# Two-layer graph convolution with lookups: seven chunks of uneven size in place of five, embeddings multiplied during the histogram, base numbers in parts

## The chip, the cores and the metric

The program runs on one core of a Trainium2 chip. The metric is the device time of one execution in microseconds, lower is better.

## The reference, cut to what matters

There are 25,000 nodes with 64 features, 250,000 edges, and 102,400 lookups. The graph is random, both endpoints uniform.

```python
def gcn_conv(x, W, b, row, col, n):
    h = x @ W
    deg = in_degree(col) + 1                  # with the node's own loop
    norm = rsqrt(deg)[row] * rsqrt(deg)[col]  # over edges and loops
    return segment_sum(h[row] * norm[:, None], col, n) + b
h1 = gcn_conv(emb, W1, b1, row, col)          # 64 -> 128
lookup = gcn_conv(h1, W2, b2, row, col)       # 128 -> 64
y = lookup[r_input]
```

## The kernel before

Since nothing nonlinear stands between the layers, W1 and W2 are multiplied first (`w12`, 64 x 64), and both rounds of aggregation work on 64 features. A round gathers, for each edge, a row of a table in DRAM (`table`) and adds it into its target node in `acc`, which holds all nodes in SBUF: 196 tiles of 128 nodes, in 98 blocks of two tiles. To add by matmul, the edges are first sorted by block of their target. The edges lie as 125 partitions x 2000 columns; a "batch" of sorting is 8 columns (1000 edges).

The stages:

1. **Histogram** (L459 to L484 on ScalarE, L616 on TensorE, `digit_rows` on VectorE). For 250 batches, one-hot rows of the targets' high and low digits are made, five of eight columns' low rows by VectorE (L864) and three as sign rows by ScalarE (L463), and TensorE multiplies them (L600). This gives in-degrees and, from columns counted apart, the number of edges of each block in each column of a chunk.
2. **Base numbers** (L896 to L987, VectorE). Prefix sums over blocks for all five chunks (L912), the order of visits, the seeds of the ranks (L1007), and the roots of the degrees.
3. **Sorting.** A chunk is 50 batches (`CB`). For each batch VectorE makes block one-hots (`block_onehots`), TensorE ranks edges within blocks (`rank_before`, `rank_rest`), VectorE takes the least (`least_ranks`, L1022) and makes partition one-hots and, for each of 8 columns, a column one-hot 488 wide (`column_onehot`, L1048, `CV` = 488) in a ring of four (`TRING`). ScalarE scales the partition one-hots by two digits of the source (`scale_column`, L497). TensorE places them (`place_column`, L600, 125 x 488): two matmuls for each column, a signal (`columns_placed`) after each. At the end of a chunk `decode` and two rounds of matmuls (`turn_sources`, `pick_tiles`) turn PSUM into gather indices (`source`, L1123) and targets.
4. **Embeddings.** While chunk 0 is sorted, TensorE also multiplies embT by `w12` (L759), VectorE scales by the root of the degree (L1147), and SP writes `table[0]`.
5. **Visits.** A chunk has 391 tiles of 128 sorted edges, gathered by GpSimd, one indirect DMA per tile (L399), in batches of 8 into a ring of 16 batches (`gath`). A tile whose edges belong to two blocks is visited for each, so a chunk has up to 391 + 97 visits, 61 batches of 8 (`VB`). A visit is a target one-hot (L1059 on VectorE, L504 and L508 on ScalarE for three of eight in round 0 up to the last chunk), TensorE's product with the tile (L702, four matmul instructions), and VectorE's addition into the block (L1069). PE signals each visit (`visits_multiplied`). The planned place of each visit is read into registers from `visits`, which SP loads once. GpSimd gathers batch n only when the visits of batch n-3 of its chunk's count are done (L416, `LAG`), and TensorE waits until the tiles of a whole batch of visits have landed, which SP counts (L350).

In round 0 the visits of chunk c run beside the sorting of chunk c+1 (`both`). After chunk 0, six batches are sorted alone (`AHEAD`) while GpSimd fills its ring. 11 batches of visits per chunk run without sorting, in the last sorted chunk 17, and the 61 of chunk 4 run alone, together with the constants (L929) and ScalarE's scaling and writing of `table[1]` (L571, L575). Round 1 is 5 x 61 batches of visits. At the end GpSimd fetches 800 tiles of lookups (L432), and SP writes them out.

Of the kernel before, what the change touches and what calls it, by code (L numbers as in the profile page):

```python
# [9 lines left out]
U8 = mybir.dt.uint8  # L10
ALU = mybir.AluOpType
# [17 lines left out]
CHUNKS = 5  # L29
W8 = 8  # L30
CB = EC // CHUNKS // W8


GB = -(-(EC // CHUNKS * EP) // (P * W8))
GT = GB * W8
CV = -(-(-(-(EC // CHUNKS * EP) // P) + NB - 1) // W8) * W8
VB = CV // W8
# [10 lines left out]
STEPS = 4  # L48
LOOPED = 11
# [5 lines left out]
CREDIT = 8  # L55
VISIT_CREDIT = 2 * W8
ADD_CREDIT = 2 * W8
TRING = 4
# [5 lines left out]
TURN = 2  # L64
AHEAD = 6
# [11 lines left out]
SHARE = 4  # L77

# [3 lines left out]

assert NT % ET == 0 and CV <= RW and CB * W8 * CHUNKS == EC and CB + TURN < VB and GROUPS % 2 and (VB - GROUPS) % 2 == 0 and CHUNKS * VB % 2 and NB == HIGH and BN == LOW
assert OUT_GROUPS * OUT_GROUP == OUT_TILES and OUT_SLOTS * OUT_GROUP <= NT
assert P * NT // NIBBLE + 1 <= HALF and NIBBLE * LOW == CODE and VB <= GB + LAG and GB == CB - 1 and RANKS <= 512 and W8 % SHARE == 0
assert all(t * RECIPROCAL >> 18 == t // RINGT for t in range(CHUNKS * GT)) and CHUNKS * GT * RECIPROCAL < 1 << 23
assert max(HISTW, CHUNKS * SLOTS) <= RINGT * FEAT - SLOTS and HBUF * HIGH <= 2 * NT and RINGT <= P and CHUNKS * GB * P < 1 << 15
assert CV * P < MARK and MARK // P % RW == 0
assert CB % 2 == 0 and GROUPS == CB - 1 and LOOPED * STEPS + 4 == CB - 2


def dve_rank(k):

    return k - sum(m < k for m in ON_ACT)


def build(nc, r_input, edge_index, embT, W1T, b1, W2, b2, out):

    with ExitStack() as ctx:  # L99
# [9 lines left out]
        visits_dram = nc.dram_tensor("visits_dram", [2, CHUNKS, P * VP], I32).ap()  # L109

# [8 lines left out]
        counts = scratch[:, 0:CHUNKS * SLOTS].bitcast(F32)  # L119
# [5 lines left out]
        edge_lo = acc[:, 128:128 + 2 * EC // (2 * FEAT) + 1, :].bitcast(F16).rearrange("p t f -> p (t f)")[:, 0:2 * EC]  # L125
        ramp = sb("ramp", [P, RW], F16)
        order = sb("order", [P, BN], F16)
        zeros_f = scratch[:, RINGW - SLOTS:RINGW].bitcast(F32)
# [9 lines left out]
        lo_half = acc[:, 160:192, :].rearrange("p t f -> p (t f)")[:, 0:EC]  # L138
        ones_f = acc[:, 16:18, :].rearrange("p t f -> p (t f)")
# [140 lines left out]
        act_onehots = sem("act_onehots")  # L280
        distances = sem("distances")

        gathered = [sem(f"gathered_{which}") for which in ("even", "odd", "last")]


        landed_of = [sem(f"landed_of_{r}") for r in range(2)]
# [1016 lines left out]
```

## Time and profile before

| what | value |
|---|---|
| median of 3 executions | 9087.14 us (9071.83 to 9087.93) |
| the profiled execution's own time | 9114.78 us |
| its span, first to last instruction | 9103.6 us |
| busy over the span | PE 61%, POOL 50%, DVE 44%, ACT 26% |
| histogram / base numbers / sorting of chunk 0 | 303 / 44 / 335 us |
| first gather, first visit | 713 us, 899 us |
| round 0 from its first visit, round 1, lookups | 3620, 3471, 1114 us |

A row of a view by stages gives the stretch, its length, then each engine's busy time and its count of instructions in it, then TensorE's granted clock (1.0 is 2.4 GHz, 0.5 is 1.2 GHz), the DMA engines' share and GB/s. PEld is TensorE's loading of weights, which overlaps its matmuls. In a view by lines, "output<-inputs shape xcount | busy us, mean ns of one | idle time of the engine before them, and what ended it". "remote" and "issue" are idle time for which the profile shows no releaser.

### The profile page before, as it was taken

What the parts mean: (1) busy time and instruction counts of PE and PEld (TensorE: products, weight loads), DVE (VectorE), ACT (ScalarE), POOL (GpSimd) and SP (SyncE); (2) the same over time, 40 slices, a digit from 0 to 9 for tenths busy, and PEclk for the clock granted to TensorE, in tenths of its full rate; (3) what the DMA queues carried; (4) which work ended last, traced back from release to release, by engine and by line L of the source; (5) the groups of instructions that cost most, each with busy time, mean ns of one, the idle gap of its engine ahead of it and who ended that gap; (6) DMA issues with size and microseconds to landing.
All of it is one profiled execution on the core that took longest, in us unless ns stands there. A gap on an engine that the chain in (4) does not pass through costs nothing. (4 is left out here: it accounts for less than half of the span.)

```text
span 9103.6 us, 134830 instructions
## 1 busy us (share of the span) xinstructions
PE 5542.4 (61%) x27534; PEld 4657.6 (51%) x27535; DVE 4024.4 (44%) x13873; ACT 2331.4 (26%) x6635; POOL 4595.8 (50%) x4740
## 2 busy tenths in 40 slices
PE   8893877777777687676645576576675675700000
PEld 6441655555655555665645575575575575700000
DVE  9872755655555465354434443343343343400000
ACT  9772754655555465200000000000000000100000
POOL 0005356355355535635346536646636636467777
PEclk9996876877777687555555555555555555555555
DMA  0011011011001100111101101101101101111111
GB/s 10 14 40 20 11 19 22 11 19 20 13 19 19 20 13 19 22 23 28 25 15 21 21 14 22 22 14 22 22 14 22 22 20 30 25 46 50 46 47 45
DMA packets 203343, 211.00 MB, mean 23 GB/s; under 512 B 81404, under 2 KB 119046, under 8 KB 203200
## 3 DMA queue, kind: packets, MB, share of 16 engines
q0 software_dynamic: 151040, 154.97, 8.6%
q1 hardware_dynamic: 25360, 41.62, 1.3%
q10 hardware_dynamic: 26800, 12.88, 0.5%
q8 instruction: 44, 0.72, 0.0%
q14 instruction: 99, 0.81, 0.0%
HBM read 163.62 MB, written 45.54 MB: 23 GB/s over the span
## 5 line engine op out<-in xcount | busy, mean ns | idle before, releaser
L399 POOL DMA_INDIRECT scratch<-table,source x3920 | 3743.9, 955 | 4137.2 <-PE ps L702 1908.7
L702 PEld LDWEIGHTS ps<-scratch,late 128*128 128x128 f32 x19520 | 3988.4, 295 | 2015.3 <-issue 1866.5
L702 PE MATMUL ps<-scratch,late 128*128 x19520 | 4013.5, 379 | 1640.0 <-issue 980.9
L1069 DVE TENSOR_TENSOR acc<-acc,ps 128x128 f32 x4880 | 1371.4, 281 | 1852.9 <-issue 754.9
L1059 DVE TENSOR_SCALAR late<-order,target 128x256 f32<-128x256 f16 x4148 | 1524.5, 368 | 959.3 <-issue 787.8
L600 PE MATMUL ps<-late 125*128 125x488 f16 x4000 | 1316.4, 420 | 612.9 <-DVE late L1048 365.3
L497 ACT ACTIVATE late<-prt_onehot,scratch 125x128 f16<-125x128 f16 x4000 | 1253.2, 388 | 1140.2 <-remote 681.6
L1048 DVE TENSOR_SCALAR late<-ramp,tcol 125x488 f16<-125x488 f16 x2000 | 685.0, 349 | 817.4 <-remote 667.2
L432 POOL DMA_INDIRECT acc<-lookup,scratch x800 | 847.5, 1059 | 352.1 <-issue 243.7
L571 ACT ACTIVATE acc<-acc,dinv (+1 forms) x196 | 57.5, 340 | 3428.1 <-DVE acc L1069 3375.3
L600 PEld LDWEIGHTS ps<-late 125*128 125x128 f16 x4000 | 420.9, 128 | 719.9 <-DVE late L1048 346.8
L508 ACT ACTIVATE late<-distance,one_col 128x256 f32<-128x256 f16 x732 | 371.7, 508 | 472.3 <-remote 261.3
L504 ACT ACTIVATE distance<-order,target 128x256 f16<-128x256 f16 x732 | 362.7, 496 | 5.7 <-issue 0.5
L463 ACT ACTIVATE scratch<-ramp,acc 125x257 f16<-125x257 f16 x750 | 300.4, 503 | 0.2
L600 PE MATMUL ps<-scratch,hi_onehot 125*98 125x265 f16 x2000 | 280.4, 283 | 22.6 <-ACT dec L470 2.1
L1022 DVE TENSOR_REDUCE place_i<-ps 125x8 int32<-125x784 f32 x250 | 242.3, 969 | 98.9 <-PE ps L600 47.5
L600 PEld LDWEIGHTS ps<-scratch,hi_onehot 125*98 125x98 f16 x2000 | 216.7, 125 | 86.5 <-DVE hi_onehot L864 86.2
L864 DVE TENSOR_TENSOR prt_onehot<-ramp,prt 125x512 f16<-125x512 f16 x500 | 208.5, 417 | 39.5 <-issue 32.9
L571 ACT ACTIVATE acc<-acc,dtmp (+1 forms) x196 | 57.5, 340 | 596.1 <-DVE acc L1069 526.5
L864 DVE TENSOR_TENSOR scratch<-ramp,acc 125x1280 f16<-125x1280 f16 x250 | 204.8, 819 | 0.2 <-issue 0.2
L600 PE MATMUL ps<-blk_onehot,before 125*128 125x392 bf16 x500 | 166.4, 425 | 44.6 <-issue 38.1
L600 PE MATMUL ps<-blk_onehot,after 125*128 125x392 bf16 x500 | 140.2, 366 | 52.0 <-DVE place_i L1022 46.0
(139 smaller groups left out, 1144.4 us busy)
## 6 DMA issues: line engine op xcount, KB each, us to landing
scratch<-table,source POOLq DMA_INDIRECT x3920
out<-acc SPq DMA_DIRECT2D x40, 640.0 KB
acc<-lookup,scratch POOLq DMA_INDIRECT x800
late<-embT SPq DMA_DIRECT2D x49, 128.0 KB, 2.6
table<-acc SPq DMA_DIRECT2D x49, 128.0 KB, 2.2
table<-acc ACTq DMA_DIRECT2D x49, 128.0 KB
lookup<-acc ACTq DMA_DIRECT2D x49, 128.0 KB
acc<-edge_index SPq DMA_DIRECT2D x2, 875.0 KB
```

Source lines behind the costliest of these rows:

```text
L399: pool.indirect_dma_start(out=place, out_offset=None, in_=table[r], in_offset=bass.IndirectOffsetOnAxis(ap=source[:, t:t + 1], axis=0)).th ...
L432: pool.indirect_dma_start(out=out_rows[:, h, k, :], out_offset=None, in_=lookup, in_offset=bass.IndirectOffsetOnAxis(ap=ask_i[:, t:t + 1], ...
L463: act.activation(lo_rows[0:EP, b, j, 0:LOW + 1], ramp[0:EP, 0:LOW + 1], ACT.Sign, bias=lo_half[0:EP, bass.ds(s * W8 + j, 1)], scale=-1.0). ...
L497: act.activation(piece[0:EP, k, j, :], prt_onehot[0:EP, b, j, :], ACT.Copy, scale=digit[k][0:EP, bass.ds(s * W8 + j, 1)]).then_inc(pieces_ ...
L504: act.activation(distance[:, 0:BN], order[:, :], ACT.Abs, bias=target[:, bass.ds(g * W8 + k, 1)], scale=-1.0).then_inc(distances, 1)
L508: act.activation(target_onehot[:, odd * W8 + k, :], distance[:, 0:BN], ACT.Relu, bias=one_col[:, 0:1], scale=-1.0).then_inc(act_onehots, 1)
L600: return pe.matmul(dst, lhsT, rhs, start=False, stop=False, skip_group_check=True)
L702: last = pe.matmul(visit_ps[odd * W8 + k][:, n * FEAT:(n + 1) * FEAT], target_onehot[:, odd * W8 + k, n * P:(n + 1) * P], row, start=True, ...
L864: return dve.tensor_tensor(place.rearrange("p j (w r) -> p j w r", r=2), of_row.rearrange("p (w r) -> p w r", r=2).unsqueeze(1).broadcast_ ...
L1048: dve.tensor_scalar(tcol_onehot[E, j % TRING, :], ramp[E, 0:CV], tcol[E, b, j:j + 1], None, ALU.is_equal).then_inc(tcol_onehots, 1)
L1059: dve.tensor_scalar(target_onehot[:, odd * W8 + k, :], order[:, :], target[:, bass.ds((g - r * BATCHES) * W8 + k, 1)], None, ALU.is_equal) ...
L1069: dve.tensor_tensor(dst, dst, visit_ps[odd * W8 + k].rearrange("p (n f) -> p n f", f=FEAT), ALU.add).then_inc(visits_added, 1)
```

## The change

- **Chunks.** Seven of 24, 32, 32, 32, 40, 40 and 50 batches (`SORTED`) in place of five of 50. Tiles, gather batches and visit batches follow for each (`TILES`, `GBS`, `VBS`): 188, 250, 250, 250, 313, 313 and 391 tiles; 24, 32, 32, 32, 40, 40 and 49 batches of gathers; 36, 44, 44, 44, 52, 52 and 61 batches of visits. Only real tiles are gathered. The placing matmuls, column one-hots and the decode chain are `WIDTH[c]` = 288, 352, 416 or 488 columns wide.
- **Order.** Chunk 0 is sorted alone, then 6 batches of chunk 1, and the rest beside visits; after each later chunk 4 to 12 batches of visits run without sorting (`VISITS_AFTER`).
- **Embeddings.** TensorE multiplies units of 8 tiles in the histogram, one per 8 batches (`multiply_unit`), ScalarE copies them to `acc` (`copy_unit`), and in each span of 8 batches one sign row moves from ScalarE to VectorE. VectorE scales the table in 14 parts of 14 tiles while chunk 0 is sorted (`scale_table`, after batches 2 to 15), and SP writes them.
- **Base numbers** are worked out chunk by chunk in ten parts (`base_numbers`): those of chunk 0 inside the histogram, those of chunk c+1 while chunk c is sorted. The block counts go through DRAM and are spread to all partitions by a broadcasting DMA in place of matmuls. The visit tables of chunks 1 to 6 are stored and loaded from ScalarE's queue.
- **Signals.** `columns_placed` and `visits_multiplied` now rise once per four columns or visits, `pieces_ready` once per pair of pieces; the ring of column one-hots has eight places, and VectorE and ScalarE wait once per four columns.
- **Landings.** TensorE waits for the landing of tiles once for each half of a batch of visits.

```diff
-CHUNKS = 5
 W8 = 8
-CB = EC // CHUNKS // W8
...
+SORTED = (24, 32, 32, 32, 40, 40, 50)
+CHUNKS = len(SORTED)
+SORT0 = [sum(SORTED[:c]) for c in range(CHUNKS)]
+BATCHED = sum(SORTED)
+
+TILES = [-(-n * W8 * EP // P) for n in SORTED]
+GBS = [-(-t // W8) for t in TILES]
+GB0 = [sum(GBS[:c]) for c in range(CHUNKS)]
+GATHERS = sum(GBS)
+VBS = [-(-(t + NB - 1) // W8) for t in TILES]
+VB0 = [sum(VBS[:c]) for c in range(CHUNKS)]
+BATCHES = sum(VBS)
+GT = max(TILES)
+WIDTH = [n * W8 for n in VBS]
...
-CREDIT = 8
-VISIT_CREDIT = 2 * W8
+HALF8 = W8 // 2
+CREDIT = 2
+VISIT_CREDIT = 2 * W8 // 4
 ADD_CREDIT = 2 * W8
-TRING = 4
+TRING = 8
...
+FIRST_ALONE = 6
+VISITS_AFTER = (0, 4, 8, 10, 8, 8, 12)
+ALONE = sum(SORTED[1:]) - FIRST_ALONE + sum(VISITS_AFTER)
+UNIT = 4
+UNITS = -(-NB // UNIT)
+SPAN = 8
...
+SCALED = 14
...
+            for u in range(UNITS):
+                if u > 0:
+                    sp.wait_ge(emb_multiplied, u)
+                for h in range(2):
+                    first = (unit_block(u) + h * (NB // 2)) * BN
+                    sp.dma_start(emb_sb[h * FEAT:(h + 1) * FEAT, :], embT[:, first:first + UNIT * P]).then_inc(emb_loaded, 16)
+                if u == COUNTS_SPAN:
+                    sp.wait_ge(counts_made, 1)
+                    spread_counts(0, 1)
+                if u == BASE_SPAN:
+                    sp.wait_ge(base_step, BASE_STEPS)
+                    for a in range(2):
+                        sp.dma_start(visits_dram[a, 0].rearrange("(p k) -> p k", p=P), visit_at[:, a, 0:VP]).then_inc(visits_stored, 16)
+                    sp.wait_ge(visits_stored, 16 * 2)
+                    sp.dma_start(visits[:, 0:VBS[0] * W8], visits_dram[:, 0, 0:VBS[0] * W8]).then_inc(visits_loaded, 16)
...
+                    for k in range(real_tiles(n)):
+                        gather(gath[:, (n % RINGB) * W8 + k, :], n * W8 + k, batch)
...
+            def copy_unit(u, n):
+
+                act.wait_ge(emb_multiplied, u + 1)
+                act.copy(acc[:, :, :].rearrange("p (s t) f -> p s t f", s=2)[:, :, bass.ds(n, UNIT), :],
+                         emb_ps.rearrange("p (q s f) -> p s q f", s=2, f=FEAT)).then_inc(emb_copied, 1)
...
                 for k in range(2):
-                    act.activation(piece[0:EP, k, j, :], prt_onehot[0:EP, b, j, :], ACT.Copy,
-                                   scale=digit[k][0:EP, bass.ds(s * W8 + j, 1)]).then_inc(pieces_ready, 1)
+                    made = act.activation(piece[0:EP, k, j, :], prt_onehot[0:EP, b, j, :], ACT.Copy,
+                                          scale=digit[k][0:EP, bass.ds(s * W8 + j, 1)])
+                made.then_inc(pieces_ready, 1)
...
+                act.wait_ge(base_step, (c + 1) * BASE_STEPS + (2 if c == CHUNKS - 1 else 0))
+                for a in range(2):
+                    act.dma_start(visits_dram[a, c].rearrange("(p k) -> p k", p=P),
+                                  visit_at[:, a, c * VP:(c + 1) * VP]).then_inc(visits_stored, 16)
+                for k in range(VISITS_AFTER[c]):
+                    visit_batch(g + k, k % 2)
+                    if k == 0:
+                        act.wait_ge(visits_stored, 2 * 16 * (c + 1))
+                        act.dma_start(visits[:, VB0[c] * W8:(VB0[c] + VBS[c]) * W8], visits_dram[:, c, 0:VBS[c] * W8]).then_inc(visits_loaded, 16)
+                g += VISITS_AFTER[c]
+                act.wait_ge(decode_step, (c + 1) * DEC)
...
+            def multiply_unit(u):
+
+                pe.wait_ge(emb_loaded, u * 32 + 32)
+                pe.wait_ge(emb_copied, u + 1)
+                nodes = emb_sb.rearrange("f (g p h) -> f g h p", p=P, h=BT)
+                for q in range(UNIT):
+                    last = pe.matmul(emb_ps[:, q * 2 * FEAT:(q + 1) * 2 * FEAT], nodes[:, q // BT, q % BT, :], w12[:, :],
+                                     start=True, stop=True)
+                last.then_inc(emb_multiplied, 1)
...
-                pe.wait_ge(pieces_ready, s * (2 * W8) + (2 * j + 2 + PIECE_CREDIT))
+            def place_column(s, j, c):
+                pe.wait_ge(pieces_ready, s * W8 + (j + 1 + PIECE_CREDIT))
                 pe.wait_ge(tcol_onehots, s * W8 + (j + 1))
                 for k in range(2):
-                    last = add(place_ps[k], piece[0:EP, k, j, :], tcol_onehot[0:EP, j % TRING, :])
-                last.then_inc(columns_placed, 1)
+                    last = add(place_ps[c][k], piece[0:EP, k, j, :], tcol_onehot[0:EP, j % TRING, 0:WIDTH[c]])
+                if j % HALF8 == HALF8 - 1:
+                    last.then_inc(columns_placed, 1)
 
             place_of = [pe.alloc_register(f"place_of_{k}") for k in range(W8)]
-            needed = pe.alloc_register("needed")
+            needed = [pe.alloc_register(f"needed_{h}") for h in range(2)]
...
-                pe.reg_alu(needed, place_of[W8 - 1], (1 << 15) - P, ALU.bitwise_and)
-                pe.reg_alu(place_of[W8 - 1], place_of[W8 - 1], P - 1, ALU.bitwise_and)
-
-            def wait_landed(r):
-                pe.wait_ge(landed_of[r], needed)
+                for h in range(2):
+                    end = place_of[h * VP + VP - 1]
+                    pe.reg_alu(needed[h], end, (1 << 15) - P, ALU.bitwise_and)
+                    pe.reg_alu(end, end, P - 1, ALU.bitwise_and)
...
+                if k % VP == 0:
+                    pe.wait_ge(landed_of[r], needed[k // VP])
...
+            def scale_table(k):
+
+                tiles = slice(k * SCALED, (k + 1) * SCALED)
+                if k == 0:
+                    dve.wait_ge(emb_copied, UNITS + 1)
+                dve.tensor_tensor(acc[:, tiles, :], acc[:, tiles, :], dinv[:, tiles].unsqueeze(2).broadcast_to([P, SCALED, FEAT]),
+                                  ALU.mult).then_inc(table_scaled, 1)
...
+            def base_numbers(c, part):
+
+                n = [c * BASE_STEPS + BASE_AT[part]]
+                if part > 0:
+                    dve.wait_ge(base_step, n[0])
...
+            digit_spans(0, COUNTS_SPAN)
+            dve.wait_ge(counts_copied, 2)
+            dve.tensor_tensor(counted[:, 0, :], summed[:, 0, 0, :], summed[:, 1, 0, :], ALU.add).then_inc(counts_made, 1)
+            digit_spans(COUNTS_SPAN, BASE_SPAN)
+            for k in range(BASE_PARTS):
+                base_numbers(0, k)
+            dve.wait_ge(rank_zeroed, 1)
+            seed_ranks(0)
+            digit_spans(BASE_SPAN, BATCHED // SPAN)
...
+            def column_onehot(s, j, b, c):
+
+                if j % HALF8 == 0:
+                    dve.wait_ge(columns_placed, s * 2 + (j // HALF8 + 1))
+                dve.tensor_scalar(tcol_onehot[E, j % TRING, 0:WIDTH[c]], ramp[E, 0:WIDTH[c]], tcol[E, b, j:j + 1], None,
...
+                parts = BASE_PARTS if more else 0
+                half = (end - s - 2 - parts) // 4 * 2
+                if half > 0:
+                    with dve.Fori(0, half // 2) as i:
+                        for b in range(2):
+                            both(s + i * 2 + b, c, b, g + i * 2 + b, b)
+                for k in range(parts):
+                    both(s + half + k, c, k % 2, g + half + k, k % 2)
+                    base_numbers(c + 1, k)
```

## Rows read from the trace of the kernel before

**Rows 1.** The page: busy time of each engine in all

```profile
PE 5542.4 (61%) x27534; PEld 4657.6 (51%) x27535; DVE 4024.4 (44%) x13873; ACT 2331.4 (26%) x6635; POOL 4595.8 (50%) x4740
```

**Rows 2.** Busy time of each engine by stage (us, count of instructions, clock)

```profile
17.00:320.00 303.00, 280.10 (x1996) 216.28 (x1995) 302.95 (x500) 301.57 (x760) 0.00 (x0) 1.00 0.00 0
320.00:364.00 44.00, 10.50 (x41) 5.69 (x38) 39.54 (x63) 6.25 (x11) 0.00 (x0) 0.69 0.01 1
364.00:699.00 335.00, 320.98 (x1498) 148.28 (x1496) 250.37 (x808) 242.51 (x809) 0.00 (x0) 0.99 0.13 38
699.00:713.00 14.00, 8.51 (x20) 4.61 (x20) 7.18 (x16) 2.21 (x8) 0.00 (x0) 0.63 0.00 0
713.00:899.00 186.00, 44.20 (x133) 12.38 (x132) 30.88 (x94) 31.00 (x93) 122.19 (x128) 0.57 0.12 23
899.00:4519.00 3620.00, 2651.99 (x14092) 2140.18 (x14090) 2004.98 (x7318) 1680.55 (x4752) 1776.13 (x1841) 0.72 0.10 19
4519.00:7990.00 3471.00, 2225.38 (x9760) 2129.56 (x9760) 1380.93 (x5063) 57.34 (x196) 1845.61 (x1951) 0.50 0.10 20
```

**Rows 3.** The same view of L702's matmuls alone, in stretches of visits

```profile
1666.80:1761.60 94.80, 54.18 (x384) 56.42 (x383) 1.00 0.00 0
1790.10:2122.10 332.00, 130.18 (x768) 145.07 (x769) 0.78 0.10 19
...
4519.30:4692.60 173.30, 30.60 (x129) 31.69 (x129) 0.50 0.12 23
4692.60:4767.70 75.10, 75.10 (x354) 75.10 (x354) 0.50 0.01 2
5469.70:6005.00 535.30, 327.54 (x1408) 308.88 (x1409) 0.50 0.12 22
```

**Rows 4.** All engines, in two of these stretches of round 0

```profile
1666.80:1761.60 94.80, 91.69 (x649) 69.91 (x647) 88.63 (x335) 87.19 (x259) 0.45 (x1) 1.00 0.00 0
1790.10:2122.10 332.00, 244.52 (x1297) 179.32 (x1297) 188.29 (x673) 184.33 (x529) 184.89 (x192) 0.78 0.10 19
```

**Rows 5.** What L399 waited for (us, times), and L702

```profile
L399 POOL DMA_INDIRECT scratch<-table,source x3920: 938/944/2088, 713.1 to 7885.5; - x196
...
  PE ps L702: 1908.7, 260
  issue: 1144.7, 3537
...
  SPq L355: 4.0, 2
```

**Rows 6.** VectorE in order of time, at 7400 us and at 7656 us

```profile
7400.00 0.29 DVE L1069 TENSOR_TENSOR acc<-acc,ps 128x128 f32 x1 [0.51 <-remote]
7400.26 0.35 DVE L1059 TENSOR_SCALAR late<-order,target 128x256 f32<-128x256 f16 x1
...
7655.91 0.35 DVE L1059 TENSOR_SCALAR late<-order,target 128x256 f32<-128x256 f16 x1 [1.87 <-issue]
```

**Rows 7.** Groups by line: count, busy, mean ns, idle before and releaser

```profile
L1048 DVE TENSOR_SCALAR late<-ramp,tcol 125x488 f16<-125x488 f16 x2000 | 685.0, 349 | 817.4 <-remote 667.2 <-PE ps L600 118.0 <-issue 31.6
...
L600 PE MATMUL ps<-scratch,hi_onehot 125*98 125x265 f16 x2000 | 280.4, 283 | 22.6 <-ACT dec L470 2.1
...
L864 DVE TENSOR_TENSOR scratch<-ramp,acc 125x1280 f16<-125x1280 f16 x250 | 204.8, 819 | 0.2 <-issue 0.2
...
L864 DVE TENSOR_TENSOR hi_onehot<-ramp,scratch 125x784 f16<-125x784 f16 x250 | 140.0, 560 | 0.0
...
L902 DVE TENSOR_TENSOR seed<-identity,dec 98x784 f32<-98x784 f32 x5 | 4.5, 970 | 0.0
```

**Rows 8.** VectorE in order of time, two rank minima after chunk 0

```profile
713.23 0.97 DVE L1022 TENSOR_REDUCE place_i<-ps 125x8 int32<-125x784 f32 x1
...
718.16 0.97 DVE L1022 TENSOR_REDUCE place_i<-ps 125x8 int32<-125x784 f32 x1 [0.26 <-PE ps L600]
```

**Rows 9.** Groups by line from 1666.8 to 1761.6 us, shapes apart

```profile
L600 PE MATMUL ps<-late 125*128 125x488 f16 x192 | 55.4, 369 | 0.0
```

More of the change, by code:

```diff
@@ L281, in build @@
         distances = sem("distances")
-        gathered = [sem(f"gathered_{which}") for which in ("even", "odd", "last")]
+        gathered = [[sem(f"gathered_{which}_{r}") for which in ("even", "odd")] for r in range(2)]
         landed_of = [sem(f"landed_of_{r}") for r in range(2)]
@@ new lines, in _ @@
+            columns(0, 0)
+            act.wait_ge(deg_step, 1)
+            act.activation(dtmp[:, :], deg[:, :], ACT.Sqrt).then_inc(root_taken, 1)
+            columns(1, 1)
+            with act.Fori(1, SORTED[0] // 2) as i:
+                for b in range(2):
+                    columns(i * 2 + b, b)
+            g = 0
+            for c in range(1, CHUNKS):
+                s, end = SORT0[c], SORT0[c] + SORTED[c]
+                if c == 1:
+                    with act.Fori(0, FIRST_ALONE // 2) as i:
+                        for b in range(2):
+                            columns(s + i * 2 + b, b)
+                    s += FIRST_ALONE
+                    act.wait_ge(decode_step, DEC)
+                with act.Fori(0, (end - s) // 2) as i:
+                    for b in range(2):
+                        both(s + i * 2 + b, b, g + i * 2 + b, b)
+                g += end - s
+                act.wait_ge(base_step, (c + 1) * BASE_STEPS + (2 if c == CHUNKS - 1 else 0))
[9 more added lines that the diff above has]
+                act.wait_ge(decode_step, (c + 1) * DEC)
@@ L626, in _, with count_span @@
+            def count_span(i, with_unit):
+                for k in range(SPAN):
+                    count_batch(i * SPAN + k, k % HBUF, i * SIGNS + min((k + 1) * BY_SIGN, SIGNS), first=BY_ONEHOT + (k == FEW))
+                    if with_unit and k == SPAN // 2 - 1:
+                        multiply_unit(i)
             for c in range(CHUNKS):
@@ L831, in _, with visits_alone @@
+            def visits_alone(r, first, count):
+                with pe.Fori(0, count // 2) as i:
+                    for b in range(2):
+                        plain_batch(r, i * 2 + (first + b), (first + b) % 2, alone=True)
+                if count % 2:
+                    plain_batch(r, first + count - 1, (first + count - 1) % 2, alone=True)
+            visits_alone(0, ALONE, BATCHES - ALONE)
+            visits_alone(1, BATCHES, BATCHES)
         @block.vector
         def _(dve):
[L833 removed]
+            dve.sem_inc(emb_copied, 1)
```

799 lines of the change are left out of this document (375 added, 424 removed).

## Prediction

> **What bounds the kernel now.** I read the page first, then its span cut into stages, then the visit stages cut again by what GpSimd does in them.
>
> The page [rows 1] names no single bound: TensorE is busy 61% of the span, GpSimd 50%, VectorE 44%; so I cut the span [rows 2]. TensorE's granted clock is 1.0 in the histogram and 0.5 in round 1 there. Histogram, 303 us: VectorE (302.95) and ScalarE (301.57) are both full. Base numbers, 44 us: VectorE alone works. Sorting chunk 0, 335 us for 50 batches, 6.7 us each: TensorE is busy 321 us, VectorE 250, ScalarE 242.5, so TensorE, which also multiplies the embeddings here, sets the pace. Then 14 us of decoding, and 186 us from the first gather to the first visit. Visits of round 0 take 3620 us, those of round 1 3471, and the lookups 1114.
>
> The two visit stages are 78% of the span, and they have two paces. Where GpSimd is silent, a batch that sorts and visits takes 94.8 / 12 = 7.90 us, and TensorE, VectorE and ScalarE are all above 90% busy at full clock; a batch of visits alone takes 75.1 / 11 = 6.83 us with TensorE busy the whole time at clock 0.5 [rows 3, 4]. (A batch of visits is 32 matmuls of L702: 384 in the first window are 12 batches. I placed the windows on first matmuls of batches.) Where GpSimd issues one batch of 8 gathers per batch of visits, the same work takes 332 / 24 = 13.83 us and 535.3 / 44 = 12.17 us [rows 3]. So 8 gathers cost 5.93 us beside sorting (0.74 each) and 5.34 us beside visits alone (0.67 each). It isn't GpSimd's own pace that shows: in the round's loop it sits idle 1909 us for TensorE [rows 5]. It is VectorE: while gathers are being issued it sits idle 1.87 us before an instruction, with nothing recorded that it waits for, where otherwise instructions start 0.26 us apart [rows 6], and TensorE runs dry behind it.
>
> The model that I use: time of a visit stage = batches x their quiet pace + gathers x their surcharge + what chunk ends cost. Check on round 1: 305 x 6.83 + 1832 gathers beyond the first 128 x 0.67 = 2083 + 1227 = 3310, plus 173 us for the first four batches, in place of 4 x 6.83 = 27: 3456, against 3471 measured.
>
> **The change, part by part.** Counts come from the constants in the code. Per round, batches of visits go from 5 x 61 = 305 to 36 + 3 x 44 + 2 x 52 + 61 = 333, since every chunk pays up to 97 visits for tiles that two blocks share. Tiles gathered go from 3920 / 2 = 1960 to 1955. Sorting stays at 250 batches, but 24 + 6 = 30 of them stand alone instead of 56, and 220 run beside visits instead of 194. Of round 0's visits 113 batches run without sorting, before 111.
>
> *Histogram, 303 us.* One batch in eight compares 6 instead of 5 rows by one-hot on VectorE. 1280 elements take 0.82 us, 784 take 0.56 [rows 7], 0.52 ns per element, so 256 more cost 0.13 us, 31 times: 4 us. ScalarE drops 31 sign rows and copies 25 units of 512 elements: about even. TensorE has room for the embeddings: 2000 matmuls take 280 of 303 us, and its clock is 1.0. Base numbers of chunk 0 and its seeds now stand in the middle: five chunks' worth and the roots are 39.5 us of VectorE [rows 2], so about 8 us for one chunk, 9.5 with the seeds. Two more chunk boundaries, and ScalarE's copies now before the next chunk: 1 to 2 us each. Sum +20 (bounds +12 and +35): 323 us.
>
> *Base numbers and roots, 44 us.* Only the in-degree sums and the first rank remain ahead of sorting; from VectorE's first group step to the first rank some 6 us: -38.
>
> *Sorting chunk 0.* Without embeddings TensorE no longer leads. ScalarE needs 242.5 / 50 = 4.85 us per batch [rows 2], and the first batches after chunk 0, which have no embeddings, come 4.9 us apart (713.23 and 718.16) [rows 8]. VectorE needs 250.4 / 50 = 5.0, less 0.42 of scaling, less the narrowed columns: 200 x 0.52 ns x 8 = 0.83; 3.75 remains. Into its 1.2 us of slack per batch go 14 scalings of 896 elements (784 take 0.97 us [rows 7]; 15 us in all), roots 3.5 us and base numbers 8 us: 26.5 against 24 x 1.2 = 29. So 24 x 5.0 + 4 = 124 us, -211. If that cover is gone, these 26 us are added. TensorE's clock could drop here, since it has 3 us of work in 5; at half clock its 6 us would lead, +24.
>
> *Decode, 14 us.* Seven dependent steps and two rounds of matmuls on 288 instead of 488 columns: 10 us, -4.
>
> *Ring fill, 186 us.* GpSimd issues 128 gathers in a row, 0.94 us each and 1144.7 / 3537 = 0.32 between them [rows 5], some 160 us, and everyone else crawls: 6 batches of sorting, 30 us of work, fill the 186. The same 128 gathers and 6 batches remain: 182, -4 (bounds -16 and +10).
>
> So the first visit comes at 899 + 20 - 38 - 211 - 4 - 4, about **662: -237 us**.
>
> *Round 0, 3620 us.* 26 more batches that sort and visit, x 7.90 = +205; two more of visits alone, +14; 5 fewer gathers, -4. Narrower columns: 90 batches at 352 and 80 at 416 instead of 488. VectorE saves 8 x 136 x 0.52 ns = 0.57 us and 0.30 per batch; TensorE, by the slope between 265 and 488 columns (283 ns [rows 7] and 369 ns [rows 9], 0.39 per column), 16 x 136 x 0.39 ns = 0.84 and 0.45. ScalarE, 87.2 / 12 = 7.27 us per batch [rows 4], saves nothing, so a batch can fall from 7.90 no further than 7.27. I take 0.45 and 0.35: -68 (bounds 0 and -100). Signals for four columns at once, and eight column one-hots in the ring instead of four: VectorE was held 118 us before these one-hots for TensorE [rows 7], 0.47 us per batch. I take 0.3 x 220 = -66. The upper bound is a rival below. Base numbers of five later chunks, now between the visits on the fullest engine: 5 x 8 = 40, +45 with their dependent steps (bounds 0, hidden behind TensorE, and 100, if each of their 25 steps takes the crawling pace of [rows 6]). Two more chunk ends, where loops change and the decode chain stands: +15 each. The tables of visits now come by ScalarE's queue: behind its wait stand the next act one-hots, but 4 us of landing lie under a visit batch of 7 to 14. Sum **+156 us** (bounds -150 and +300).
>
> *Round 1, 3471 us.* 28 more batches, x 6.83 = +191. These are quiet batches, because the count of gathers stays and each chunk still has 12 to 13 batches more than gathers: no stall covers them. 5 fewer gathers, -3. Waiting for landings by halves: in both rounds TensorE was idle for the landings' counter 4 us in all [rows 5], so I take -4. It also adds register work on TensorE, which isn't late. Coarser signals leave VectorE's waits in number as they are; I take -4. **+180 us.**
>
> There is one rule for the coarser signals. TensorE runs 354 matmuls in 75.1 us, 0.212 us each, one in four with a signal, without a gap [rows 3]. The Trainium skill (TensorE: Matmul & The Clock Gate, section on the per-tile semaphore tail) says that signals of TensorE serialize, at 26 ns each; by that, 6 fewer per visit batch would be an estimated 0.16 us, 53 us per round. The trace shows only back-to-back matmuls, which neither confirms nor denies it.
>
> *Lookups, 1114 us*: untouched.
>
> Sum: -237 + 156 + 180 = **+99 us**. The profiled execution's own time is 9114.8, 27.6 us above the median of 9087.1; 9114.8 + 99 - 27.6 = **9186**. The two rounds pay 28 batches each for an earlier start that comes only once.
>
> **The rivals.** A change under 0.2% (18 us) can't be told from none here.
>
> *A. The crawl beside sorting shrinks (faster).* In batches with gathers TensorE is idle 87.5 of 332 us, 3.6 per batch, and its clock averages 0.78 [rows 4]. With eight one-hots ready instead of four it could work through the crawl and keep its clock. About 139 batches of round 0 are of this kind. If 13.83 falls to 11.6 where I take 13.1, that is 139 x 1.5 = -209: 8977. It decides from 0.7 us per batch beyond mine (99 / 139). For: TensorE does run dry just there. Against: what is late is VectorE, which has 7.3 us of work per batch and loses 5 to 6; it was held for TensorE only 0.47 us.
>
> *B. Signals cost TensorE time.* As a mechanism of this kernel: if part of the 0.212 us is the signal, 6 of 8 fall away in each visit batch, and 6 of 8 in sorting. 0.1 to 0.16 us x 666 and x 250 is 90 to 145 us: 9041 to 9096. Against it: the even spacing.
>
> *C. The extra batches are free*, because the gathers bound the rounds (1955 x 1.26 = 2460 us of issue per round). Then round 1 stays: 9006. Against: GpSimd's 1909 us of idling for TensorE.
>
> *D. The middle parts lose more:* sorting at half clock, base numbers at the crawling pace, code outside loops. +24, +55, +30: 9295.
>
> **How the numbers follow.** The forecast, with its own range 9110 to 9260, 0.54; D 0.13; A 0.15; B 0.05; C 0.05; all in between, within 18 us of no change, 0.08. Slower by over 0.2%: 0.67; within: 0.08; faster: 0.25. Range: the bounds of round 0 and the ring fill reach down to A's upper half and up to D: 9010 to 9290.
>
> **What would show it.** The first gather at about 480 instead of 713, the first visit at about 662. Quiet batches of visits alone still 6.83 us, now about 13 per chunk in seven chunks, and round 1 about 3650 us. Quiet sorting batches of 7.4 to 7.6 us in chunks 1 to 3, 13.1 us with gathers. Sorting of chunk 0 at 5.0 us per batch with clock 1.0. I am wrong if batches with gathers come below 12.4 us beside sorting or below 11.6 in round 1, or if round 1 grows by much less than 28 quiet batches.

## The result and the profile after

The changed kernel takes 9135.97 us (median of 5, 9120.04 to 9148.71) beside 9086.65 us for the kernel before (5 runs): ratio 1.0059, 95% interval 1.0043 to 1.0075. It is slower by 49 us, where +99 was forecast. The profiled execution has a span of 9124.7 us, 21.1 more than before: it is a run at its kernel's median, where the profiled run of the kernel before took 27.6 us more than the median of its first three runs. So the stages below add up to some 20 us and not to 49, and by them the forecast was about 80 us too high and not 50.

The page's busy line, as [rows 1]:

```profile
PE 5636.0 (62%) x29150; PEld 4965.3 (54%) x29151; DVE 4165.2 (46%) x14817; ACT 2374.8 (26%) x6785; POOL 4592.1 (50%) x4730
```

Again it names no bound. The stages by windows, as [rows 2]; columns are the window, its length, busy time and count of TensorE, its weight loads, VectorE, ScalarE and GpSimd, then TensorE's clock, DMA share and GB/s:

```profile
17.00:340.00 323.00, 290.11 (x2208) 248.04 (x2208) 318.66 (x534) 302.87 (x762) 0.00 (x0) 0.98 0.07 21
343.00:480.00 137.00, 95.46 (x533) 47.09 (x532) 126.64 (x414) 117.00 (x390) 0.00 (x0) 0.92 0.19 56
480.00:682.00 202.00, 39.88 (x151) 18.08 (x152) 34.00 (x111) 31.37 (x104) 121.46 (x128) 0.56 0.11 21
682.00:4434.00 3752.00, 2814.09 (x15597) 2321.82 (x15595) 2207.85 (x8235) 1855.94 (x5327) 1776.16 (x1837) 0.72 0.09 18
4434.00:8009.00 3575.00, 2394.62 (x10656) 2329.35 (x10656) 1468.18 (x5508) 56.91 (x194) 1843.27 (x1946) 0.50 0.10 20
```

The reader sees histogram, sorting of chunk 0, decode with ring fill, and the two rounds. Against the forecast:

| | before | forecast | after |
|---|---|---|---|
| histogram | 303 | 323 | 323 |
| base numbers ahead of sorting | 44 | 6 | 3 |
| sorting chunk 0 | 335 | 124 | 137 |
| decode and ring fill | 200 | 192 | 202 |
| first visit at | 899 | 662 | 682 |
| round 0 | 3620 | 3776 | 3752 |
| round 1 | 3471 | 3651 | 3575 |

The start gave 217 us, not 237; round 0 cost 132, not 156; round 1 cost 104, not 180. The paces of stretches, as [rows 3, 4] (a batch of visits is 32 matmuls). Seven windows: five that sort while GpSimd is silent (eleven, ten, eleven, eleven and eleven batches; columns 352, 352, 416, 416 and 488 wide), then two with gathers (nineteen batches, and eleven):

```profile
1140.70:1227.80 87.10, 77.06 (x596) 61.70 (x594) 84.30 (x326) 82.28 (x244) 0.00 (x0) 1.00 0.00 0
1639.50:1717.50 78.00, 69.81 (x542) 56.12 (x541) 75.13 (x295) 75.10 (x224) 0.00 (x0) 1.00 0.00 0
2129.60:2217.90 88.30, 81.60 (x595) 63.68 (x594) 86.51 (x332) 82.94 (x245) 0.00 (x0) 1.00 0.00 0
2636.40:2724.00 87.60, 80.53 (x597) 63.40 (x595) 84.80 (x320) 82.72 (x245) 0.00 (x0) 1.00 0.00 0
3239.30:3324.90 85.60, 83.63 (x597) 64.32 (x595) 81.35 (x307) 81.64 (x241) 0.00 (x0) 1.00 0.00 0
...
2744.90:2987.70 242.80, 185.40 (x997) 144.63 (x997) 143.01 (x523) 134.84 (x387) 147.53 (x152) 0.75 0.11 21
...
1955.80:2098.10 142.30, 112.09 (x596) 84.98 (x595) 84.41 (x310) 82.87 (x244) 85.05 (x90) 0.76 0.11 20
```

Quiet sorting batches take 7.92, 7.80, 8.03, 7.96 and 7.78 us, 7.90 over all five, as before (7.90), not 7.45. In the first two TensorE has come down to 88 and 90% busy (it was 97% in [rows 4]) and VectorE is at 97 and 96%; in the last, which sorts the 488-wide chunk, TensorE is at 98% and VectorE at 95%. With gathers a batch takes 242.8 / 19 = 12.78 us, forecast 13.1. Two of these nineteen sort nothing (135 column one-hots are 17 batches); where all eleven sort it is 142.3 / 11 = 12.94. Visits alone, a quiet stretch and the start of round 1, which took 173.3 us before [rows 3]:

```profile
3852.00:3927.10 75.10, 75.10 (x354) 75.10 (x354) 57.12 (x236) 11.36 (x39) 0.00 (x0) 0.50 0.05 16
...
4433.90:4608.00 174.10, 32.41 (x135) 33.20 (x135) 13.84 (x56) 0.00 (x0) 111.99 (x119) 0.50 0.12 23
4689.20:4929.40 240.20, 146.26 (x640) 139.55 (x640) 105.34 (x396) 0.00 (x0) 150.89 (x159) 0.50 0.11 22
```

The quiet pace is the same 6.83 us (75.1 / 11) with two signals a batch as it was with eight. With gathers it is 240.2 / 20 = 12.01.

One thing is new: two batches of visits behind chunk 1's end took 58.1 and 22.3 us. TensorE in order of time there (start, duration, line, tiles, idle time before and what ended it; L762 is the visits' matmul, L702 before):

```profile
952.05 0.27 PE L762 MATMUL ps<-scratch,late 128*128 x1 [1.24 <-issue]
954.16 0.26 PE L762 MATMUL ps<-scratch,late 128*128 x1 [1.84 <-issue]
...
962.56 0.26 PE L762 MATMUL ps<-scratch,late 128*128 x1 [3.25 <-issue]
965.35 0.26 PE L762 MATMUL ps<-scratch,late 128*128 x1 [2.52 <-issue]
968.14 0.27 PE L762 MATMUL ps<-scratch,late 128*128 x1 [2.53 <-issue]
```

And GpSimd just before it (L440 gathers a tile, L1191 makes the indices `source`):

```profile
938.46 0.94 POOL L440 DMA_INDIRECT scratch<-table,source  x1 [54.03 <-DVE source L1191]
...
939.71 0.94 POOL L440 DMA_INDIRECT scratch<-table,source  x1 [0.30 <-issue]
```

GpSimd had gathered all of chunk 0 (24 batches) and sat idle 54 us until chunk 1's sources came; then it issued without a pause, and from about 13 us later TensorE's matmuls come 1.4 to 3.5 us apart instead of 0.2, with nothing recorded that they wait for. The start of round 1 looks alike: in the 174.1 us shown above TensorE is busy 32.4 us while GpSimd issues 119 gathers.

### The profile page after: what moved, and what is told of

Read it like the earlier page. It is cut to its first block and busy times, and to the rows that moved or that the text cites. A ratio compares the mean times of both kernels' runs of the same rounds, so it can differ in the third digit from the quotient of the medians.

```text
span 9124.7 us, 138318 instructions
## 1 busy us (share of the span) xinstructions
PE 5636.0 (62%) x29150; PEld 4965.3 (54%) x29151; DVE 4165.2 (46%) x14817; ACT 2374.8 (26%) x6785; POOL 4592.1 (50%) x4730
## 3 DMA queue, kind: packets, MB, share of 16 engines
q10 hardware_dynamic: 28552, 12.93, 0.5%
## 5 line engine op out<-in xcount | busy, mean ns | idle before, releaser
L440 POOL DMA_INDIRECT scratch<-table,source x3910 | 3740.9, 957 | 4172.5 <-PE ps L762 1726.4
L762 PEld LDWEIGHTS ps<-scratch,late 128*128 128x128 f32 x21312 | 4325.3, 294 | 2143.3 <-issue 2026.0
L762 PE MATMUL ps<-scratch,late 128*128 x21312 | 4361.5, 376 | 1803.4 <-issue 1358.6
L1136 DVE TENSOR_TENSOR acc<-acc,ps 128x128 f32 x5328 | 1497.1, 281 | 2096.4 <-issue 1227.0
L1126 DVE TENSOR_SCALAR late<-order,target 128x256 f32<-128x256 f16 x4518 | 1629.5, 361 | 710.9 <-issue 626.8
L650 PE MATMUL ps<-late 125*128 125x352 f16 (+3 forms) x4000 | 1143.1, 376 | 165.6 <-issue 90.4
L1115 DVE TENSOR_SCALAR late<-ramp,tcol 125x352 f16<-125x352 f16 (+3 forms) x2000 | 638.2, 323 | 171.0 <-remote 116.7
L556 ACT ACTIVATE late<-distance,one_col 128x256 f32<-128x256 f16 x810 | 411.3, 508 | 493.7 <-remote 316.2
L905 DVE TENSOR_TENSOR blk_onehot<-ramp,scratch 125x784 bf16<-125x784 f16 x250 | 140.4, 562 | 450.3 <-remote 421.5
L506 ACT ACTIVATE scratch<-ramp,late 125x257 f16<-125x257 f16 x719 | 290.9, 505 | 10.1 <-PE ps L650 9.9
L905 DVE TENSOR_TENSOR scratch<-ramp,late 125x1280 f16<-125x1280 f16 x250 | 208.7, 835 | 0.5 <-PE ps L650 0.2
```

The lines of the kernel that those rows point to most:

```text
L440: pool.indirect_dma_start(out=place, out_offset=None, in_=table[r], in_offset=bass.IndirectOffsetOnAxis(ap=source[:, t:t + 1], axis=0)).th ...
L506: act.activation(lo_rows[0:EP, b, j, 0:LOW + 1], ramp[0:EP, 0:LOW + 1], ACT.Sign, bias=lo_half[0:EP, bass.ds(s * W8 + j, 1)], scale=-1.0). ...
L556: act.activation(target_onehot[:, odd * W8 + k, :], distance[:, 0:BN], ACT.Relu, bias=one_col[:, 0:1], scale=-1.0).then_inc(act_onehots, 1)
L650: return pe.matmul(dst, lhsT, rhs, start=False, stop=False, skip_group_check=True)
L762: last = pe.matmul(visit_ps[odd * W8 + k][:, n * FEAT:(n + 1) * FEAT], target_onehot[:, odd * W8 + k, n * P:(n + 1) * P], row, start=True, ...
L905: return dve.tensor_tensor(place.rearrange("p j (w r) -> p j w r", r=2), of_row.rearrange("p (w r) -> p w r", r=2).unsqueeze(1).broadcast_ ...
```

## The experiments

Ratios are to the kernel before, with 95% intervals. Stages come from each profiled run, placed on the first matmul of a batch, and are set beside the profiled runs of the first two kernels. Read their small differences with care: the medians of the kernel before lie between 9084.8 and 9104.2 us, depending on the chip, and one kernel profiled on two chips (the six chunks below) differs by 10 us in round 0 and by 3 in round 1.

### Which part of round 1's extra gain is it?

Round 1 grew by 104 us and not by 180 although its quiet pace is as forecast. VectorE's records hold a hint. In quiet visit batches the trace of before has 7.4 register operations a batch that work out the value of the wait ahead of a target one-hot (81 in eleven batches); after has 1.1 (12 in eleven), since four waits in a row now have one value. The prediction had said "leave VectorE's waits in number as they are".

**Coarse visit signals alone, on the kernel before**

```diff
-                last.then_inc(visits_multiplied, 1)
+                if k % SHARE == SHARE - 1:
+                    last.then_inc(visits_multiplied, 1)
...
-                dve.wait_ge(visits_multiplied, g * W8 + (k + 1 + VISIT_CREDIT - RING))
+                dve.wait_ge(visits_multiplied, g * 2 + (k // SHARE + 1 + VISIT_CREDIT - RING // SHARE))
```

> The kernel before with one part of the change alone: TensorE signals its visits once per four instead of once each, and VectorE, ScalarE and GpSimd count in fours (everything else as before). Theory A (what round 1 gained beyond the forecast is VectorE's wait values: one value worked out per half batch in place of one per visit, each a record that costs most of a microsecond's tenth in the quiet and far more while GpSimd issues gathers): round 1 falls by about 80 us (a batch beside eight gathers from 12.2 to 11.9 us), round 0 by 50 to 100 us, the quiet pace of 6.83 us stays; the whole 8930 to 8960, ratio 0.983 to 0.987. Theory B (the landings by halves gave it): no change, ratio 0.998 to 1.002. Theory C (TensorE pays for each signal): the quiet pace falls too, by up to 0.16 us a batch, and the whole by another 100 us.

Measured: 9030.9, ratio 0.9919 (0.9902 to 0.9936). Round 1 3397.6, that is 71 less than in the kernel before measured the same way (3468.2); round 0 13 less, where 50 to 100 was expected; quiet pace unchanged. Theory A holds for round 1; its size for round 0 was wrong, and so the whole gained less than 0.983 to 0.987. Theory C (the quiet pace falls too) fails.

**Landings by halves alone, on the kernel before**

```diff
-                pe.wait_ge(landed_of[r], needed)
+                if k % VP == 0:
+                    pe.wait_ge(landed_of[r], needed[k // VP])
```

> The kernel before with the landings by halves alone: TensorE waits for the tiles of a batch's first four visits before the first and for those of its last four before the fifth, where before it waits for all eight at the start. Theory A (VectorE's wait values): within 0.2% of before, a few us at the start of a round and nothing in the paced stretches. Theory B (the halves gave what round 1 gained): round 1 shorter by about 80 us, ratio about 0.99.

Measured: 9128.2, ratio 1.0023 (1.0012 to 1.0033). Round 1 3466.3, unchanged; round 0 3640.9, 21 more. The halves gave nothing and cost a little, a trifle more than the 0.2% that theory A allowed. Theory B falls.

**Equal wait values alone, on the kernel before, all signals kept**

```diff
-                dve.wait_ge(visits_multiplied, g * W8 + (k + 1 + VISIT_CREDIT - RING))
+                dve.wait_ge(visits_multiplied, g * W8 + (k // SHARE * SHARE + SHARE + VISIT_CREDIT - RING))
```

> The kernel before, TensorE still signalling every visit, but VectorE's wait ahead of a target one-hot uses one value for four visits (the last of the four that held the same place in the ring), so the value is worked out once per half batch. Theory A (VectorE's wait values are the cost): the same gain as with the coarse signals to within 0.3%, ratio 0.983 to 0.990, with seven fewer register records per batch on VectorE. Theory C (TensorE's signals are the cost): no change, since TensorE signals as before. Theory B (halves): no change.

Measured: 9046.5, ratio 0.9934 (0.9917 to 0.9951). The gain is within 0.3% of that of the coarse signals, but smaller than the 0.983 to 0.990 expected. Round 1 3411.7, 57 of the 71 us; round 0 3603.4, 17 less; VectorE's register operations at this wait 1.05 a quiet batch. TensorE signals as before here, and the new wait values ask for no less than the old ones, so the gain is VectorE's, from register operations that are gone. In round 1 these are 302 instead of 2114; 57 us over 1812 of them is about 31 ns each, an estimate (the median of one in the trace is 40 ns). Some 14 us is left for TensorE's signals, about what two runs can differ by.

**The changed kernel with fine visit signals**: the first edit the other way round.

> The changed kernel with its visit signals made fine again (one per visit, and the waits counted in ones), all else as changed. Theory A: slower than the changed kernel by 130 to 180 us, so 9270 to 9310, ratio to before 1.020 to 1.025; round 1 at about 3655, as the prediction had it. Theory B (the halves gave it): 9136 as the changed kernel, ratio 1.005.

Measured: 9225.4, ratio 1.0135 (1.0118 to 1.0152), 0.76% above the changed kernel. Round 1 3633.5 (+59), round 0 3785.1 (+33). The direction is A's; the size is about half of what I wrote (130 to 180 us) by the ratios, 69 us, and under two thirds by the stages, 92 us.

### What do narrow columns and coarser column signals give?

**All columns 488 wide, in the changed kernel**

```diff
-                dve.tensor_scalar(tcol_onehot[E, j % TRING, 0:WIDTH[c]], ramp[E, 0:WIDTH[c]], tcol[E, b, j:j + 1], None,
+                dve.tensor_scalar(tcol_onehot[E, j % TRING, :], ramp[E, 0:CV], tcol[E, b, j:j + 1], None,
```

(and the same width in the column matmuls)

> The changed kernel with every column one-hot and every column matmul 488 wide again (the width of the last chunk), all else as changed. The prediction (narrow columns save 68 us of round 0, 0.45 us in a quiet sorting batch): round 0 at about 3820, the whole 9205. Rival, from the quiet sorting batches that stayed at 7.9 us: narrow columns save nothing there, so only batches with gathers pay; round 0 grows by 0 to 30 us, the whole 9136 to 9165.

Measured: 9159.7, ratio 1.0081 (1.0064 to 1.0098). Round 0 3779.9, 28 more, as the rival had it; the first quiet window 8.09 us a batch instead of 7.92. Narrow columns are worth some 28 us, not 68. The quiet windows of this kernel also show what the base numbers cost, since all its columns are 488 wide: 8.09, 7.99, 8.13 and 8.05 us a batch where they stand between the visits, 7.78 in the last, where none are left. That is some 3 us for each such window, and an estimated 15 us for the five chunks, where +45 was taken; their steps between batches with gathers are not in it.

**Column signals one by one, in the changed kernel**

```diff
-                if j % HALF8 == HALF8 - 1:
-                    last.then_inc(columns_placed, 1)
+                last.then_inc(columns_placed, 1)
```

(VectorE and ScalarE then wait for each column)

> The changed kernel with the signals of the columns made fine again (TensorE signals each column, VectorE and ScalarE wait for each; the ring of eight and all else as changed). If waits with a value to work out cost their share here too (12 more such records a batch on VectorE and ScalarE, in 226 sorting batches of round 0 and 24 alone): round 0 grows by 30 to 50 us, ratio to before 1.009 to 1.011. Rival, they lie beside other work in round 0: within 0.2% of the changed kernel.

Measured: 9155.6, ratio 1.0079 (1.0062 to 1.0096). Round 0 3772.0, 20 more. By the medians the two expectations can't be told apart; round 0 points to some 20 us, which is not shown beyond doubt: in the kernel with ScalarE's part short, below, which has no cause to be slower, round 0 is 18 us longer too.

**Who sets the pace of a quiet sorting batch?** Two kernels that leave a part of the one-hots out:

```diff
-                act.activation(distance[:, 0:BN], order[:, :], ACT.Abs, ...
+                act.activation(distance[:, 0:64], order[:, 0:64], ACT.Abs, ...
```

> The changed kernel in which ScalarE works out the distances of its target one-hots for 64 columns instead of 256 (the other 192 keep a fixed value, so this part of the computation is left out): three activations of 0.51 us a batch become shorter by about 0.15 to 0.3 us each. If ScalarE sets the pace of the quiet sorting batches (8.0 us), they fall to 7.2 to 7.5 us. If VectorE or TensorE sets it, they stay at 8.0.

```diff
-                dve.tensor_scalar(target_onehot[:, odd * W8 + k, :], order[:, :], ...
+                w = BN if alone else 64
+                dve.tensor_scalar(target_onehot[:, odd * W8 + k, 0:w], order[:, 0:w], ...
```

> The changed kernel in which VectorE makes its five target one-hots of a sorting batch 64 columns wide instead of 256 (the rest is zero, so this part of the computation is left out): five operations of 0.36 us become shorter by about 0.15 to 0.2 us each, 0.75 to 1 us a batch. If VectorE sets the pace of the quiet sorting batches (8.0 us), they fall to 7.0 to 7.4 us; if ScalarE or TensorE sets it, they stay.

The first quiet window, eleven batches, by engines as above. With ScalarE's part short:

```profile
1139.10:1226.30 87.20, 77.12 (x597) 61.80 (x595) 84.28 (x326) 77.57 (x244) 0.00 (x0) 1.00 0.00 0
```

With VectorE's part short:

```profile
1139.50:1223.30 83.80, 75.82 (x596) 61.56 (x594) 80.68 (x326) 80.75 (x241) 0.00 (x0) 1.00 0.00 0
```

ScalarE lost 4.7 us of work and the window stayed at 87.2; VectorE lost 3.6 and the window lost 3.3. VectorE sets the pace there. In the last quiet window, 488 wide, it does so only in part: VectorE lost 3.3 us and the window 1.5 (85.6 to 84.1), with TensorE busy 83.3 of it. (VectorE's target one-hots shrank by 0.07 us each, not 0.15, so the pace fell to 7.62 and not to 7.0 to 7.4.) With gathers the batches stayed (19 batches at 12.89), and the whole took 9133.6, one run, 1.004 of the kernel before on that chip: hardly less than the changed kernel, since few batches are quiet. The one with ScalarE's part short took 9160.5, one run, 1.007 of it.

What VectorE does in that window of the changed kernel, by line (busy us, mean ns, idle before; L1115 is the column one-hot, L951 to L988 are base numbers):

```profile
L1115 DVE TENSOR_SCALAR late<-ramp,tcol 125x352 f16<-125x352 f16 x87 | 26.4, 304 | 0.0
...
L951 DVE TENSOR_TENSOR_SCAN dec<-seed,zero_col 128x784 f32<-128x784 uint16 x1 | 1.8, 1781 | 0.0
L963 DVE SCALAR_TENSOR_TENSOR seed<-dec 128x784 uint16<-128x784 f32 x1 | 1.0, 966 | 0.0
L968 DVE TENSOR_TENSOR dec<-dec,visit_no 128x392 f32<-128x392 f32 x1 | 0.6, 566 | 0.0
L974 DVE TENSOR_TENSOR dec<-dec 128x392 f32<-128x392 f32 x1 | 0.6, 559 | 0.0
```

And its column one-hots in eleven quiet batches of the kernel before (1666.8 to 1753.4):

```profile
L1048 DVE TENSOR_SCALAR late<-ramp,tcol 125x488 f16<-125x488 f16 x87 | 29.6, 340 | 0.0
```

A column one-hot takes 304 ns at 352 wide where it took 340, which saves 29.6 - 26.4 = 3.2 us in the window. The parts of the base numbers stand in the same window, 22 instructions of 8.4 us in all, of which the four shown take 4.0 us. One edit filled the room that the other had made.

### What do the chunks cost?

**Six chunks**

```diff
-SORTED = (24, 32, 32, 32, 40, 40, 50)
-VISITS_AFTER = (0, 4, 8, 10, 8, 8, 12)
+SORTED = (32, 32, 40, 48, 48, 50)
+VISITS_AFTER = (0, 4, 8, 10, 8, 12)
```

(`COUNTS_SPAN`, the span of the histogram after which chunk 0's counts are complete, goes from 3 to 4 with a first chunk of 32)

> The changed kernel with six chunks of 32, 32, 40, 48, 48 and 50 batches instead of seven: 319 visit batches a round instead of 333, sorting of chunk 0 eight batches longer. Theory of the prediction (a visit batch more costs its quiet pace, 7.9 us in round 0 and 6.83 in round 1; the stall of 80 us behind the short chunks 0 and 1 is part of that price): +40 for chunk 0, -110 in round 0, -96 in round 1, so 8960 to 8990, ratio 0.985 to 0.990. Rival (the loss comes from elsewhere in the change, the short start of the ring and the middle parts): 9050 to 9100.

Measured: 8969.1, ratio 0.9868 (0.9852 to 0.9885), as expected. First visit 720.7 (+38), round 0 3618.7 (-133, 110 expected), round 1 3501.2 (-74, 96 expected): the two misses of some 22 us cancel. In round 1 a batch less gave 5.3 us, not 6.83. No batch of chunk 0's visits takes over 17.1 us.

**Six chunks, the first short**: SORTED = (24, 32, 48, 48, 48, 50), VISITS_AFTER = (0, 4, 2, 8, 12, 10).

> The changed kernel with six chunks of 24, 32, 48, 48, 48 and 50 batches: the first chunk as short as in the changed kernel, 318 visit batches a round. By the prediction's terms: first visit at 682 as in the changed kernel, round 0 shorter by 15 batches of 7.9 us (118), round 1 by 15 of 6.83 us (102): 8916 to 8940. Rival (the stall behind short chunks is a price of its own: chunk 0 of 24 brings 35 us more of it than chunk 0 of 32): equal to the six chunks that begin with 32, within 0.2%.

Measured: 9099.5, ratio 1.0015 (1.0006 to 1.0025). Both expectations miss by far: 318 batches, one less than the kernel above, and 130 us more. First visit and round 1 are as expected (681.5; 3488.9); round 0 is 3815.6, longer by 197 than with (32, 32, 40, ...). Single batches take 58.8, 75.0, 98.6, 55.0 and 50.5 us. GpSimd is idle 120.9 us until chunk 2's sources come, and the ring's refill then looks like this (windows by engine, before and in it):

```profile
1427.30:1549.10 121.80, 112.34 (x749) 87.66 (x746) 105.82 (x389) 107.41 (x313) 0.94 (x1) 0.93 0.01 1
1560.70:1734.30 173.60, 32.45 (x109) 21.39 (x110) 16.30 (x56) 11.36 (x33) 112.58 (x119) 0.51 0.12 23
```

In 173.6 us two batches of visits are done, with TensorE busy 32 us; it is a second start of a round. A chunk of 32 can't feed the visits while 48 batches are sorted.

**Seven chunks, the first of 32**: SORTED = (32, 32, 32, 32, 32, 40, 50), `COUNTS_SPAN` 4, the same 333 visit batches as in the changed kernel.

> The changed kernel with seven chunks of 32, 32, 32, 32, 32, 40 and 50 batches: the same 333 visit batches a round as in the changed kernel, the first chunk as long as the second. Theory (behind a first chunk of 24 GpSimd runs out of tiles 54 us before chunk 1 is decoded, and then refills the ring while two visit batches take 58 and 22 us): chunk 0 is sorted 40 us later, the stall of 66 us is gone, the other terms are as in the changed kernel: 9110, between 9095 and 9125. Rival (the stall only moves waiting that some batch has to bear anyway): 9176, later by the 40 us.

Measured: 9130.0, ratio 1.0039 (1.0025 to 1.0053), between the two but nearer to the theory; the kernel before took 9099.1 on this chip, so by the ratios it is 0.2% below the changed kernel. First visit 717.4 (+35), round 0 3708.9 (-43), no batch of chunk 0 over 16.8 us. Of the 66 us that two batches had lost (58.1 + 22.3 - 2 x 7), 43 came back in round 0; that the rest was waiting that moved elsewhere is not shown.

**Six chunks once more** (the label names an edit that this kernel does not have).

> The six chunks of 32, 32, 40, 48, 48 and 50 once more, as the kernel that the next one is compared with in its profile: 8969.

Measured: 8978.1, one run, beside 9099.1 for the kernel before on that chip, 0.987 again.

## Why the prediction was right, and where its sizes were off

The likeliest case came true: the earlier start (-217) is paid back by 28 more batches in both rounds. None of the rivals did. The sum was 50 us too high by the medians, and about 80 by the stages; the 28 us between them is how far the profiled run of the kernel before lay above its median. Some of the prediction's own signs failed all the same: quiet sorting batches stayed at 7.9 us (7.4 to 7.6 forecast), and round 1 grew by much less than 28 quiet batches, which it had named as a sign of being wrong. The experiments say why: the batches cost nearly what was forecast, and the waits gave back 59 us that the sum had at 4. That round 0 came out within 24 us is partly luck, since its terms missed in both directions.

- **Model of the rounds.** Batches at a quiet pace plus gathers at a surcharge held roughly: six chunks, computed from it, came out at 8969 where 8960 to 8990 was written, though only because its two rounds missed by some 22 us in opposite directions. With fine signals and 28 more batches, round 1 grew from 3468.2 to 3633.5, +165, where +180 to +191 was forecast; that is 5.9 us for each extra batch. By the runs with coarse signals (3397.6 to 3574.8) it is 6.3, and by the six chunks 5.3. Rival C (free) falls.
- **Round 1's signals: the step that was mis-sized most.** "Coarser signals leave VectorE's waits in number as they are; I take -4." They measured -59 in the changed kernel and -71 in the one before, of which equal wait values alone gave 57. The waits' number stays, but their values become equal, and VectorE works out one value where it worked out four. The quiet pace doesn't show it (6.83 with either), since TensorE is busy all of that time; the gain is in the batches where GpSimd issues and VectorE is late. With all of the rest of round 1 put on its gathers beyond the first 128, (round 1 - batches x 6.83) / gathers, the surcharge is 0.756 us before, 0.717 and 0.725 with coarse signals and with equal waits, 0.744 and 0.712 in the changed kernel with fine and coarse ones.
- **Rival B and the rule beside it.** Six of eight signals a batch are gone and eleven quiet batches take 75.1 us as before, so no 26 ns each can be seen here in a stream of visits. The Trainium skill (TensorE: Matmul & The Clock Gate, section on the per-tile semaphore tail) gives its 26 ns for the tail behind a group of packed tiles, each with a signal; carried over to this stream, as the prediction did in an estimate of 0.16 us a batch, it does not hold. No run here has packed tiles, so none shows the tail itself.
- **Narrow columns, -68 taken, -28 measured.** I let TensorE and VectorE save together and looked for the next limit in ScalarE's 7.27 us; ScalarE was not it, as the two kernels with short one-hots show. VectorE stood at 93% in [rows 4], and the same change put the base numbers into those batches.
- **Signals and ring of eight in round 0, -66 taken.** Visit signals gave up to 33 (13 in the kernel before) and column signals perhaps 20. Batches with gathers fell from 13.83 [rows 3] to 12.94 where all of them sort, 0.9 us where 0.7 was forecast. None of wide columns (12.93), fine column signals (12.87) or fine visit signals (12.97) brings that back in the same eleven batches of the changed kernel. What remains is the ring of eight one-hots and the pieces' signals by twos, neither of which was tried alone, and the landings by halves, which alone made round 0 longer. The cause of that 0.9 us stays open.
- **Chunk ends, +15 each.** Most are of that kind; the one behind chunk 1 cost 66 us, since chunk 0 is too short for the visits that run while chunk 1 is sorted. I had looked at what stands behind a decode, but not at when GpSimd runs out of tiles ahead of it. That round 0 came out below the forecast in spite of it was not closed into a sum. What points that way: the batches with gathers, above; the base numbers (+45 taken, an estimated 15 us in the quiet windows); and the extra batches (+205 taken, 7.9 each), since between the two kernels that begin with 32, of seven and of six chunks, 14 batches and a chunk end less gave 90 us of round 0, 6.4 a batch.
- **The start, 20 us late.** Sorting chunk 0 took 137 us and not 124: TensorE was busy 70% of it at a mean clock of 0.92, and VectorE 126.6 us, so the 26.5 us of scalings and base numbers did not fit into the slack as neatly as the sum assumed. The ring fill took 192 us and not 182.
- **Landings by halves, -4 a round taken.** Alone, in the kernel before, they left round 1 as it was and made round 0 longer by 21 us; why was not tried.

## What to carry to other kernels

Where an engine is late rather than busy, count its register operations too, not only its compute: giving four waits one value made a kernel of 9104 us faster by 58, with no other change. When work is cut into chunks, each chunk must feed its consumer for as long as the next one takes to prepare; compare these two spans for every pair, because while an empty ring was refilled here two batches of visits took 173.6 us, where two quiet ones take 14. And before a saving on one engine is booked, ask which other engine is within 5% of it and whether the same change adds work there.

## What the runs showed of the hardware

- The signal of a matmul costs nothing visible in a stream of 0.212 us matmuls: eleven batches of 32 take 75.1 us with eight signals a batch and with two.
- Four waits of VectorE with one value in place of four values are 1812 register operations fewer in round 1, and 57 us: about 31 ns each, an estimate, although VectorE is busy only 40% of that round in the kernel before [rows 2].
- Behind chunk 1's end, while GpSimd issued indirect DMAs without a pause (0.94 us each, 0.30 between), TensorE kept its pace for some 13 us and then started a matmul only every 1.4 to 3.5 us, at clock 0.5. In 70 us from there it did this:

```profile
951.00:1021.00 70.00, 10.68 (x44) 10.81 (x43) 5.52 (x21) 8.36 (x24) 45.85 (x49) 0.50 0.12 23
```

  VectorE ran 21 instructions and ScalarE 24 in that time; the trace names nothing that the three waited for. The cause was not isolated.
- TensorE's granted clock stayed at 1.0 (2.4 GHz) in the quiet sorting stretches, where it was busy 88 to 98% of the time. In the sorting of chunk 0, where it was busy 70%, the mean was 0.92.
